# First GCN layer: bias from a table on VectorE, input split on GpSimd, transposes inside the first aggregation

## The chip, the cores and the metric

One core of a Trainium2 chip runs the whole program. The metric is device time in microseconds from launch to the last store. The profile is one execution of the program, recorded by the hardware. Engines are named as the profile names them: PE is TensorE, PEld its weight load, DVE is VectorE, ACT is ScalarE, POOL is GpSimd, SP issues DMAs.

## The reference, cut to what matters

The input is `x` of 32 graphs by 256 nodes by 128 features. A graph attention layer comes first, then a layer norm, two graph convolutions and four LSTMs over windows of 1 to 4 nodes, with a residual at each half.

```python
h = jnp.maximum(_layernorm(x, axis=-1), 0.0)
x = x + _L0_gnn_ref(h, adj, L0_gnn_W, L0_gnn_a)            # attention
h = jnp.maximum(_layernorm(x, axis=-1), 0.0)
# second half:
h = jax.nn.relu(jnp.einsum('ts,bsh->bth', adj, x @ Wg0 + bg0))
h = jax.nn.relu(jnp.einsum('ts,bsh->bth', adj, h @ Wg1 + bg1))
for p in range(1, 5):      # windows of p nodes: the last step's h replaces the window's last node
    last = _lstm_last(Wih[p - 1], Whh[p - 1], bih[p - 1], bhh[p - 1], wins)
    h = h.at[:, idx, :].set(last)
return x + h
```

In the first graph convolution the kernel aggregates before it multiplies: adj (v Wg0 + b0) is (adj v) Wg0 plus b0 times the row sums of adj. That last term, b0 by row sum, is the one the change handles in another way.

## The kernel before, in words

The 32 graphs go through in 16 pairs; one pair is 512 nodes, so most tiles are 128x512. Every engine has a hand-written program, run in order, and semaphores join them. The function `ticks` gives each engine a software pipeline: in tick t, stage s works on pair t - s. `live(s)` says whether that pair exists, and `after(...)` adds the wait for a buffer that is used again.

There are three parts. Part A (`phase_a`, to about 112 us of the profile) is attention. Part B (`phase_b`) holds the two graph convolutions and the LSTM with one step; its first four ticks run beside the end of part A, and ticks 4 to 21 alone (to about 230 us). Then the LSTMs with 2, 3 and 4 steps follow. fp32 products are made from a high and a low part of each operand (names ending in `_hi` and `_lo`), three products for one (`product`, L1005).

Part B by stages, for one pair:

- Stage 0: ACT normalises the pair into `v_norm` (`second_norm`, L545, four activations at L500). DVE makes its high part with a cast (L806) and its low part with a subtraction (L808).
- Stage 1, first aggregation: PE multiplies by the adjacency (twelve 256-column products). ACT copies the high part out of PSUM (`part_hi(1)`, L590), DVE subtracts for the low part (`part_lo(1)`, L792).
- Stage 2: PE multiplies by Wg0 and adds the bias by a fourth product, `b0_parts` by `rs_parts` (L1078). ACT applies relu for the high part, DVE makes the low part from PSUM (L794).
- Stage 3: PE multiplies by Wg1; ACT adds the second bias into `y1` (L597); PE transposes `y1` (`turned`, L1046 to L1055); high and low parts again.
- Stage 4, second aggregation, into `h_hi` (ACT, L590) and `h_lo` (DVE, L794).
- Stages 5 and 6: the one-step LSTM. PE computes three gates, ACT their activations (L573) and the tanh of the cell (L566). DVE computes the cell (L776), the output by three products of 168 or 176 columns (L768), its cast (L772) and its low part (L779).

The order within one tick of part B is this. PE: gates, stages 4, 3, 2, the transposes, stage 1. ACT: tanh, the gates I, G, O, high part 4, `y1`, high part 2, high part 3, normalisation, high part 1. DVE: L768, L772, L776, L779, low part 4, low part 2, low part 3, the input's cast and subtraction, low part 1.

GpSimd computes the norm's scale and shift for 16 tiles at a time (`norm_scale`), prepares the bias and row-sum operands, and splits the LSTM weights in 14 pieces of 256 columns (`split_weights`, L457). The last 12 pieces are paced by the LSTM's progress (L476).

```python
after(dve, b_mm[1], t, 0)
nc.vector.tensor_copy(s_hi[:, 0, :], v).then_inc(b_hi[0], 1)
dve.wait_ge(b_hi[0], t + 1)
nc.vector.tensor_tensor(s_lo[:, 0, :], v, s_hi[:, 0, :].bitcast(fp32),
                        ALU.subtract).then_inc(b_lo[0], 1)
```

Of the kernel before, what the change touches and what calls it, by code (L numbers as in the profile page):

```python
# [5 lines left out]
def preln_gat_gcn_lstm_kernel(  # L6
# [28 lines left out]
    P = 128  # L35
# [15 lines left out]
    GCN_LOADS = 8  # L51
# [7 lines left out]
    with ctx:  # L59
        def sb(name, shape, dt=fp32):  # L60
            return ctx.enter_context(nc.sbuf_tensor(name, shape, dt))
# [33 lines left out]
        b_raw = sb("b_raw", [P, D])  # L95
        b_full = sb("b_full", [P, D])
        b1_col = sb("b1_col", [P, 1])
        y1 = sb("y1", [P, 512])
        b0_parts = sb("b0_parts", [P, D], fp32r)
        rs_full = sb("rs_full", [P, N])  # L100
        rs_parts = sb("rs_parts", [P, 2, N], fp32r)
# [68 lines left out]
        b_zero = sem("b_zero")  # L170
# [3 lines left out]
        rs_ok = sem("rs_ok")  # L174
# [26 lines left out]
        b_y = sem("b_y")  # L201
        b_T = sem("b_T")
# [172 lines left out]
        def _(pool):  # L375
# [11 lines left out]
            done(nc.gpsimd.memset(b_raw[:, :], 0.0))  # L387
            nc.gpsimd.nop().then_inc(b_zero, 1)
# [39 lines left out]
            nc.gpsimd.nop().then_inc(rs_ok, 1)  # L428


            pool.wait_ge(gcn_w_in, GCN_LOADS * 16)
# [3 lines left out]
            nc.gpsimd.tensor_tensor(bl[:, :], bl_raw[:, 0], bl_raw[:, 1], ALU.add)  # L435
            done(nc.gpsimd.tensor_copy(b_full[:, :].bitcast(fp32r), b_raw[:, :]))
            done(nc.gpsimd.tensor_copy(b0_parts[0:32], b_full[0:32]))
            done(nc.gpsimd.tensor_tensor(b0_parts[32:64], b_raw[32:64], b_full[32:64], ALU.subtract))
            done(nc.gpsimd.tensor_copy(b0_parts[64:P], b_full[64:P]))
# [41 lines left out]
        def _(act):  # L481
# [80 lines left out]
            def phase_b(t, ph, live):  # L562
# [13 lines left out]
                def part_hi(s):  # L576
                    if not live(s):
                        return
                    if s == 4:
                        dst = h_hi[:, bass.ds((t - 4) * PN, PN)]  # L580
                    else:
                        dst = s_hi[:, s, :]
                    if s == 3:

                        act.wait_ge(b_T, t - 2)
                    else:
                        act.wait_ge(b_mm[s], t - s + 1)
                    if s < 4:
                        after(act, b_mm[s + 1], t - s, 0)
                    nc.scalar.activation(dst, ps[:, TURNED if s == 3 else s - 1, :],  # L590
                                         ACT.Copy if s in (1, 3) else ACT.Relu).then_inc(b_hi[s], 1)
# [67 lines left out]
        def _(dve):  # L659
# [97 lines left out]
            def phase_b(t, ph, live):  # L757
# [23 lines left out]
                def part_lo(s):  # L781
# [9 lines left out]
                    if s in (1, 3):  # L791
                        ins = nc.vector.tensor_tensor(dst, ps[:, TURNED if s == 3 else 0, :], hi.bitcast(fp32), ALU.subtract)  # L792
                    else:
                        ins = nc.vector.scalar_tensor_tensor(dst, ps[:, s - 1, :], 0.0, hi.bitcast(fp32), ALU.max,  # L794
                                                             ALU.subtract)
                    ins.then_inc(b_lo[s], 1)

                part_lo(4)
                part_lo(2)
                part_lo(3)  # L800
                if live(0):

                    v = v_norm[:, :, :].rearrange("p k f -> p (k f)")
                    dve.wait_ge(b_v, t + 1)
                    after(dve, b_mm[1], t, 0)
                    nc.vector.tensor_copy(s_hi[:, 0, :], v).then_inc(b_hi[0], 1)  # L806
                    dve.wait_ge(b_hi[0], t + 1)
                    nc.vector.tensor_tensor(s_lo[:, 0, :], v, s_hi[:, 0, :].bitcast(fp32),  # L808
                                            ALU.subtract).then_inc(b_lo[0], 1)
# [125 lines left out]
        def _(pe):  # L935
# [87 lines left out]
            def phase_b(t, ph, live):  # L1023
# [33 lines left out]
                for s in (4, 3, 2, 1):  # L1057
                    if s == 1:
                        turned()
                    if not live(s):  # L1060
                        continue
                    after(pe, b_y if s == 3 else b_lo[s], t - s, 0)
# [10 lines left out]
                    if s == 2:  # L1073

                        product(ps[:, s - 1, :], (wg_hi[:, 0, :], wg_lo[:, 0, :]), (hi, lo), True, False)
                        if isinstance(t, int) and t == 2:
                            pe.wait_ge(rs_ok, 1)
                        ins = nc.tensor.matmul(ps[:, s - 1, :], b0_parts[:, :], rs_parts[:, :, :].rearrange("p b n -> p (b n)"),  # L1078
                                               start=False, stop=True)
# [3 lines left out]
                    else:  # L1083

                        for b in range(2):
                            for u in range(2):
# [130 lines left out]
```

## Time and profile before

| | |
|---|---|
| median of 3 runs | 451.97 us (450.59 to 452.68) |
| the profiled execution, time | 452.38 us |
| its span | 450.5 us |
| mean granted TensorE clock | 0.992 |
| PE busy | 430.0 us (95%) |
| DVE busy | 374.5 us (83%) |
| ACT busy | 333.0 us (74%) |
| POOL busy | 71.5 us (16%) |

The span runs from the first to the last instruction; launch and end add 1.9 us to it. Busy shares are averages over three parts of the program. The matter of this case is a stretch of some 100 us in the middle, where all engines work in step on ticks.

### The profile page before, as it was taken

Reading aid. Unit: us, or ns where it says so; the run is one execution under the profiler, and the core shown is the slowest. Engines: PE = TensorE matmul, PEld = TensorE weight load, DVE = VectorE, ACT = ScalarE, POOL = GpSimd, SP = SyncE. Lnnn points to the kernel's source line nnn. Section 1 sums busy time; section 2 is a strip of 40 time slices with the busy share of each in tenths; the row PEclk is TensorE's granted clock in tenths of the full one; section 3 lists DMA queues with packets and bytes.
Section 4 is the critical chain, followed back from the end, with each engine's and each line's share of the span. In section 5 each row is a group of like instructions: output and inputs, shape, how many; then the busy total and the mean of one; then the engine's idle time right before and its main releaser. Section 6 shows DMA issues by size and latency. Waiting matters only on the chain.

```text
span 450.5 us, 7896 instructions
## 1 busy us (share of the span) xinstructions
PE 430.0 (95%) x2472; PEld 371.4 (82%) x2472; DVE 374.5 (83%) x973; ACT 333.0 (74%) x651; POOL 71.5 (16%) x169
## 2 busy tenths in 40 slices
PE   7689999979999999999999999999999999999995
PEld 6468888878888888888778888899999988887884
DVE  3898999997778877878778888878788789888995
ACT  2579999977899999997777768757767675574552
POOL 5848640422411213110000000000000000000000
PEclk9969999999999999999999999999999999999999
DMA  8910000000000000000000000000000000002116
GB/s 244 324 65 1 2 2 1 0 0 1 1 1 2 0 1 0 0 0 0 1 0 2 1 0 1 0 1 1 1 1 1 1 1 0 1 23 71 47 47 188
DMA packets 14213, 11.68 MB, mean 26 GB/s; under 512 B 1123, under 2 KB 12390, under 8 KB 13926
## 3 DMA queue, kind: packets, MB, share of 16 engines
q1 hardware_dynamic: 11542, 9.97, 7.3%
q10 hardware_dynamic: 2640, 1.33, 1.2%
q8 instruction: 16, 0.26, 0.2%
q14 instruction: 15, 0.12, 0.1%
HBM read 7.10 MB, written 4.19 MB: 25 GB/s over the span
## 4 chain that ended last, share of the span: by engine, by line
PE 70%; DVE 18%; ACT 5%; issue 3%; DMA 2%; DVEq 1%; SPq 0%; ACTq 0%
PE ps L1008 45%; PE ps L1152 12%; PE ps L1156 6%; DVE score L732 4%; DVE score L698 4%; DVE xs L746 2%; DMA xs<-in_x 2%; PE ps L1054 2%; DVE stats L688 2%; ACT v_norm L500 1%; DVE stats L665 1%; PE ps L988 1%; ACT work L625 1%; PE ps L1099 1%; PE ps L1078 1%
## 5 line engine op out<-in xcount | busy, mean ns | idle before, releaser
L625 ACT ACTIVATE work<-ps,bl 128x512 f32<-128x512 f32 (+2 forms) x204 | 111.0, 627 | 26.7 <-PE ps L1156 19.3
L1008 PE MATMUL ps<-h_hi,wl_hi 128*128 128x512 f32 (+3 forms) x252 | 93.5, 371 | 0.9 <-DVE xs L888 0.8
L1008 PE MATMUL ps<-h_hi,wl_lo 128*128 128x512 f32 (+3 forms) x252 | 92.8, 368 | 0.0
L1008 PE MATMUL ps<-h_lo,wl_hi 128*128 128x512 f32 (+3 forms) x252 | 92.7, 368 | 0.0
L615 ACT ACTIVATE work<-work 128x512 f32<-128x512 f32 (+2 forms) x56 | 31.5, 571 | 45.5 <-DVE work L883 34.6
L1008 PEld LDWEIGHTS ps<-h_hi,wl_hi 128*128 128x128 f32 x252 | 47.5, 188 | 8.3 <-issue 1.2
L500 ACT ACTIVATE v_norm<-xs,shift,scale 128x128 f32 (+1 forms) x128 | 53.3, 509 | 1.4 <-POOL shift L409 1.4
L1008 PEld LDWEIGHTS ps<-h_lo,wl_hi 128*128 128x128 f32 x252 | 47.4, 188 | 6.6
L1008 PEld LDWEIGHTS ps<-h_hi,wl_lo 128*128 128x128 f32 x252 | 47.5, 188 | 5.7
L1152 PE MATMUL ps<-s_hi,wl_hi 128*128 128x512 f32 (+2 forms) x144 | 51.7, 361 | 0.0
L1152 PE MATMUL ps<-s_hi,wl_lo 128*128 128x512 f32 (+2 forms) x144 | 51.2, 358 | 0.0
L573 ACT ACTIVATE work<-ps,bl 128x512 f32<-128x512 f32 x48 | 30.8, 683 | 6.5 <-DVE work L768 5.2
L988 PE MATMUL ps<-wh,pT 128*128 128x130 f32 x256 | 32.6, 280 | 2.8 <-DVE xs L746 2.1
L1156 PE MATMUL ps<-s_lo,wl_hi 128*128 128x512 f32 (+2 forms) x144 | 34.4, 358 | 0.3 <-DVE s_lo L845 0.3
L988 PEld LDWEIGHTS ps<-wh,pT 128*128 128x128 f32 x256 | 29.9, 190 | 5.6 <-ACT pT L542 3.6
L590 ACT ACTIVATE s_hi<-ps 128x512 fp32r<-128x512 f32 x48 | 28.1, 593 | 5.5 <-PE ps L1078 2.1
L834 DVE TENSOR_TENSOR s_hi<-work 128x512 fp32r<-128x512 f32 (+2 forms) x36 | 22.0, 611 | 12.0 <-ACT work L615 11.1
L533 ACT ACTIVATE prob<-score,ebias 128x256 f32<-128x256 f32 x64 | 28.0, 547 | 4.6 <-DVE ebias L710 4.6
L838 DVE TENSOR_TENSOR work<-work 128x512 f32<-128x512 f32 (+2 forms) x52 | 31.3, 602 | 0.0
L1152 PEld LDWEIGHTS ps<-s_hi,wl_hi 128*128 128x128 f32 x144 | 27.1, 188 | 3.0
L1152 PEld LDWEIGHTS ps<-s_hi,wl_lo 128*128 128x128 f32 x144 | 27.1, 188 | 2.9
L1156 PEld LDWEIGHTS ps<-s_lo,wl_hi 128*128 128x128 f32 x144 | 25.4, 188 | 3.7 <-DVE s_lo L845 0.6
(127 smaller groups left out, 924.5 us busy)
## 6 DMA issues: line engine op xcount, KB each, us to landing
result<-xs SPq DMA_DIRECT2D x12, 256.0 KB, 2.3
work<-in_w_ih_t SPq DMA_DIRECT2D x1, 1024.0 KB, 10.9
work<-in_w_hh_t SPq DMA_DIRECT2D x1, 1024.0 KB, 9.4
xs<-in_x SPq DMA_DIRECT2D x2, 256.0 KB, 3.6
xs<-in_x SPq DMA_DIRECT2D x1, 512.0 KB, 5.6
result<-xs SPq DMA_DIRECT2D x4, 128.0 KB, 2.4
result<-xs ACTq DMA_DIRECT2D x4, 128.0 KB, 2.8
adj_raw<-in_adj ACTq DMA_DIRECT2D x1, 256.0 KB, 6.8
```

The source lines that it names most:

```text
L500: ins = nc.scalar.activation(v_norm[:, k, :], xs[:, bass.ds(i, 1), :].rearrange("p o f -> p (o f)"), ACT.Relu, scale=scale[:, which, bass. ...
L533: ins = nc.scalar.activation(prob[:, m, k], score[:, m, k], ACT.Exp, scale=1.0 - SLOPE, bias=ebias[:, m, k:k + 1])
L573: nc.scalar.activation(one_row(g), ps[:, 4 + g, :], ACT.Tanh if g == G else ACT.Sigmoid, bias=bl[:, g:g + 1]).then_inc(one_act, 1)
L590: nc.scalar.activation(dst, ps[:, TURNED if s == 3 else s - 1, :], ACT.Copy if s in (1, 3) else ACT.Relu).then_inc(b_hi[s], 1)
L615: nc.scalar.activation(lw[:, par, R_TC, 0:cols], lw[:, par, R_C, 0:cols], ACT.Tanh).then_inc(c_act[par], 1)
L625: nc.scalar.activation(lw[:, par, g, 0:cols], ps[:, 4 * par + g, 0:cols], ACT.Tanh if g == G else ACT.Sigmoid, bias=bl[:, (p - 1) * GATES ...
L834: nc.vector.tensor_tensor(hi, shaped(lw[:, par, O, :]), shaped(lw[:, par, R_TC, :]), ALU.mult).then_inc(c_hi[par], 1)
L838: nc.vector.tensor_tensor(row(r, par, R_H), row(r, par, O), row(r, par, R_TC), ALU.mult).then_inc(c_h[par], 1)
L988: ins = nc.tensor.matmul(psA[:, b, ui * (D + 2):(ui + 1) * (D + 2)], pT[:, 2 * b + uj, ui * P:(ui + 1) * P], wh[:, (ph - 4) % 4, 2 * b + u ...
L1008: ins = nc.tensor.matmul(dst, a, b, start=start and n_ == 0, stop=stop and n_ == 2)
L1152: nc.tensor.matmul(ps[:, 4 * par + g, 0:cols], part, s_hi[:, par, 0:cols], start=False, stop=False)
L1156: nc.tensor.matmul(ps[:, 4 * par + g, 0:cols], weights(p, 1, g)[0], s_lo[:, par, 0:cols], start=False, stop=True).then_inc(c_gate[par], 1)
```

## The change

The bias of the first graph convolution leaves TensorE. GpSimd multiplies the row sums (already the same in every partition) by the bias, one value in each partition, to a table `b0_rs` of 128x256. In each tick DVE adds the table to the product in PSUM, in two halves of 256 columns, and writes `z0`, in SBUF. ACT's high part and DVE's low part of stage 2 now read `z0`. The split of `v_norm` moves from DVE to GpSimd, where it stands between the norm's scales and the pieces of the weights, whose pacing changes. The transposes of stage 3 move from before the first aggregation to its middle, after the first graph of the pair.

```diff
-            sp.wait_ge(b_zero, 1)
-            for r in (0, 32, 64):
-                sp.dma_start(b_raw[r:r + 1, :], b_gcn0.rearrange("(o f) -> o f", o=1)).then_inc(gcn_w_in, 16)
+            sp.dma_start(b0_col[:, :], b_gcn0.rearrange("(f o) -> f o", o=1)).then_inc(gcn_w_in, 16)
...
             pool.wait_ge(rs_read, 1)
-            done(nc.gpsimd.tensor_copy(rs_full[:, :].bitcast(fp32r), rs_raw[:, :]))
-            for b in range(2):
-                done(nc.gpsimd.tensor_copy(rs_parts[0:64, b], rs_full[0:64]))
-                done(nc.gpsimd.tensor_copy(rs_parts[96:P, b], rs_full[96:P]))
-                done(nc.gpsimd.tensor_tensor(rs_parts[64:96, b], rs_raw[64:96], rs_full[64:96], ALU.subtract))
...
+            nc.gpsimd.tensor_scalar(b0_rs[:, :], rs_raw[:, :], b0_col[:, 0:1], 0.0, ALU.mult, ALU.add).then_inc(b0_rs_ok, 1)
...
-            for c in range(4):
+            def second_scale(c):
                 pool.wait_ge(stats_ok, TILES + (c + 1) * QUARTER)
                 norm_scale(1, c * QUARTER, QUARTER)
-            for n_, (p, m, c) in enumerate((p, m, c) for p in range(2, SKIPS + 1) for m in range(2) for c in range(2)):
-                pool.wait_ge(one_lo, 1 + 3 * n_ // 4)
-                split_weights(p, m, c)
+            def input_parts(q):
+
+                v = v_norm[:, :, :].rearrange("p k f -> p (k f)")
+                pool.wait_ge(b_v, q + 1)
+                if q > 0:
+                    pool.wait_ge(b_mm[1], q)
+                done(nc.gpsimd.tensor_copy(s_hi[:, 0, :], v))
+                nc.gpsimd.tensor_tensor(s_lo[:, 0, :], v, s_hi[:, 0, :].bitcast(fp32), ALU.subtract).then_inc(b_lo[0], 1)
+
+            second_scale(0)
+            second_scale(1)
+
+            pieces = [(p, m, c) for p in range(2, SKIPS + 1) for m in range(2) for c in range(2)]
+            for q in range(PAIRS):
+                input_parts(q)
+                if q in (1, 5):
+                    second_scale(2 + q // 4)
+                for n_, piece in enumerate(pieces):
+                    if 7 + 3 * n_ // 4 == q:
+                        split_weights(*piece)
...
+                    elif s == 2:
+                        act.wait_ge(b_z, t - 1)
...
                 part_lo(4)
+                if live(2):
+
+                    dve.wait_ge(b_mm[2], t - 1)
+                    if isinstance(t, int) and t == 2:
+                        dve.wait_ge(b0_rs_ok, 1)
+                    after(dve, b_lo[2], t - 2, 0)
+                    for b in range(2):
+                        c = slice(b * N, (b + 1) * N)
+                        ins = nc.vector.tensor_tensor(z0[:, c], ps[:, 1, c], b0_rs[:, :], ALU.add)
+                    ins.then_inc(b_z, 1)
                 part_lo(2)
                 part_lo(3)
-                if live(0):
-
-                    v = v_norm[:, :, :].rearrange("p k f -> p (k f)")
-                    dve.wait_ge(b_v, t + 1)
-                    after(dve, b_mm[1], t, 0)
-                    nc.vector.tensor_copy(s_hi[:, 0, :], v).then_inc(b_hi[0], 1)
-                    dve.wait_ge(b_hi[0], t + 1)
-                    nc.vector.tensor_tensor(s_lo[:, 0, :], v, s_hi[:, 0, :].bitcast(fp32),
-                                            ALU.subtract).then_inc(b_lo[0], 1)
                 part_lo(1)
...
-                        product(ps[:, s - 1, :], (wg_hi[:, 0, :], wg_lo[:, 0, :]), (hi, lo), True, False)
-                        if isinstance(t, int) and t == 2:
-                            pe.wait_ge(rs_ok, 1)
-                        ins = nc.tensor.matmul(ps[:, s - 1, :], b0_parts[:, :], rs_parts[:, :, :].rearrange("p b n -> p (b n)"),
-                                               start=False, stop=True)
+                        ins = product(ps[:, s - 1, :], (wg_hi[:, 0, :], wg_lo[:, 0, :]), (hi, lo), True, True)
...
                         for b in range(2):
+                            if (s, b) == (1, 1):
+                                turned()
```

## Rows read from the trace of the kernel before

**Rows 1.** The page, part 4: the chain that ended last, by engine.

```profile
PE 70%; DVE 18%; ACT 5%; issue 3%; DMA 2%; DVEq 1%; SPq 0%; ACTq 0%
```

**Rows 2.** Busy us by engine (count), clock, DMA: eleven ticks of part B.

```profile
126.64:206.43 79.79, 79.42 (x485) 68.04 (x485) 65.72 (x133) 72.80 (x144) 13.64 (x24) 1.00 0.00 1
```

**Rows 3.** Timeline of PE in one tick of part B (start us, us).

```profile
162.90 0.66 PE L1054 MATMUL ps<-ident,y 128*128 128x128 f32 x4
...
169.50 0.39 PE L1008 MATMUL ps<-s_lo,wg_hi 128*128 128x512 f32 x1
169.73 0.40 PE L1078 MATMUL ps<-rs_parts,b_parts 128*128 128x512 f32 x1
170.15 0.66 PE L1054 MATMUL ps<-ident,y 128*128 128x128 f32 x4
```

**Rows 4.** Timeline of PEld, same tick; in brackets idle time and its releaser.

```profile
170.15 0.42 PEld L1054 LDWEIGHTS ps<-ident,y 128*128 128x128 f32 x4 [0.46 <-ACT y L597]
```

**Rows 5.** Timeline of ACT, same tick.

```profile
164.09 1.64 ACT L500 ACTIVATE v_norm<-xs,shift,scale 128x128 f32 x4
165.63 0.58 ACT L590 ACTIVATE s_hi<-ps 128x512 fp32r<-128x512 f32 x1
166.11 0.62 ACT L566 ACTIVATE work<-work 128x512 f32<-128x512 f32 x1
...
168.93 0.59 ACT L590 ACTIVATE h_hi<-ps 128x512 f32 x1
169.41 0.69 ACT L597 ACTIVATE y<-ps,b_col 128x512 f32<-128x512 f32 x1
```

**Rows 6.** Timeline of DVE, same tick.

```profile
165.76 0.43 DVE L806 CAST s_hi<-v_norm 128x512 fp32r<-128x512 f32 x1 [0.84 <-ACT v_norm L500]
166.22 0.69 DVE L808 TENSOR_TENSOR s_lo<-v_norm,s_hi 128x512 fp32r<-128x512 f32 x1
166.83 0.68 DVE L792 TENSOR_TENSOR s_lo<-ps,s_hi 128x512 fp32r<-128x512 f32 x1
167.43 0.82 DVE L768 TENSOR_TENSOR work<-work 128x176 f32<-128x176 f32 x3
168.40 0.43 DVE L772 CAST h_hi<-work 128x512 f32 x1
168.74 0.68 DVE L776 TENSOR_TENSOR work<-work 128x512 f32<-128x512 f32 x1
```

**Rows 7.** Line L732, 64 instructions: duration in ns, min/median/max.

```profile
L732 DVE SCALAR_TENSOR_TENSOR score<-ps,wh,score x64: 460/476/486, 17.5 to 97.6; 128x256 f32<-128x256 f32 x64
```

**Rows 8.** Timeline of POOL: a cast and a subtraction of 512 columns.

```profile
21.29 0.61 POOL L417 CAST adjT_hi<-adjT_raw 128x512 fp32r<-128x512 f32 x1
21.98 1.26 POOL L418 TENSOR_TENSOR adjT_lo<-adjT_raw,adjT_hi 128x512 fp32r<-128x512 f32 x1
```

**Rows 9.** Timeline of DVE at the same time.

```profile
22.18 1.08 DVE L706 SCALAR_TENSOR_TENSOR low<-m,wh 128x4 f32<-128x4 f32 x1
```

**Rows 10.** Line L706, 16 instructions: duration in ns, min/median/max.

```profile
L706 DVE SCALAR_TENSOR_TENSOR low<-m,wh x16: 151/166/1078, 22.2 to 100.5; 128x4 f32<-128x4 f32 x16
```

**Rows 11.** Groups by line of POOL: pieces of the LSTM weights (busy, mean ns).

```profile
L461 POOL TENSOR_TENSOR wl_lo<-work,wl_hi 128x256 fp32r<-128x256 f32 x14 | 10.3, 738 | 1.1
...
L460 POOL CAST wl_hi<-work 128x256 fp32r<-128x256 f32 x14 | 5.6, 397 | 54.6 <-DVE h_lo L779 54.2 <-POOL adjP_lo L452 0.2
```

**Rows 12.** Timeline of POOL: first and last of ten instructions of one `norm_scale`.

```profile
118.84 0.24 POOL L400 TENSOR_TENSOR ln_b<-stats 128x16 f32<-128x16 f32 x1 [14.17 <-DVE stats L688]
...
123.92 0.22 POOL L409 TENSOR_TENSOR shift<-ln_c,scale 128x16 f32<-128x16 f32 x1
```

**Rows 13.** Timeline of ACT: the normalisation of pair 1.

```profile
103.53 1.63 ACT L500 ACTIVATE v_norm<-xs,shift,scale 128x128 f32<-128x128 f32 x4
```

**Rows 14.** Timeline of PE in tick 3: transposes, then first aggregation.

```profile
113.32 0.60 PE L1054 MATMUL ps<-ident,y 128*128 128x128 f32 x4
113.67 0.36 PE L1008 MATMUL ps<-adjT_hi,s_hi 128*128 128x256 f32 x1
```

More of the change, by code:

```diff
@@ L50, in preln_gat_gcn_lstm_kernel @@
     SKIPS = 4
-    GCN_LOADS = 8
+    GCN_LOADS = 6
     GATES = 4
@@ L94, in preln_gat_gcn_lstm_kernel @@
         wg_lo = sb("wg_lo", [P, 2, D], fp32r)
-        b_raw = sb("b_raw", [P, D])
-        b_full = sb("b_full", [P, D])
+        b0_col = sb("b0_col", [P, 1])
         b1_col = sb("b1_col", [P, 1])
+        b0_rs = sb("b0_rs", [P, N])
+        z0 = sb("z0", [P, 512])
         y1 = sb("y1", [P, 512])
-        b0_parts = sb("b0_parts", [P, D], fp32r)
-        rs_full = sb("rs_full", [P, N])
-        rs_parts = sb("rs_parts", [P, 2, N], fp32r)
         ones = sb("ones", [P, P], fp32r)
@@ L169, in preln_gat_gcn_lstm_kernel @@
         pool_step = sem("pool_step")
-        b_zero = sem("b_zero")
         ones_ok = sem("ones_ok")
@@ L173, in preln_gat_gcn_lstm_kernel @@
         rs_read = sem("rs_read")
-        rs_ok = sem("rs_ok")
+        b0_rs_ok = sem("b0_rs_ok")
         adjT_ok = sem("adjT_ok")
@@ L201, in preln_gat_gcn_lstm_kernel @@
         b_y = sem("b_y")
+        b_z = sem("b_z")
         b_T = sem("b_T")
@@ L386, in _ @@
                                     pattern=[[-1, P]], channel_multiplier=1).then_inc(ident_ok, 1)
-            done(nc.gpsimd.memset(b_raw[:, :], 0.0))
-            nc.gpsimd.nop().then_inc(b_zero, 1)
             nc.gpsimd.memset(wh[:, :, :, D + 2:D + 3], 1.0)
@@ L422, in _ @@
             pool.wait_ge(rs_read, 1)
-            done(nc.gpsimd.tensor_copy(rs_full[:, :].bitcast(fp32r), rs_raw[:, :]))
-            for b in range(2):
-                done(nc.gpsimd.tensor_copy(rs_parts[0:64, b], rs_full[0:64]))
-                done(nc.gpsimd.tensor_copy(rs_parts[96:P, b], rs_full[96:P]))
-                done(nc.gpsimd.tensor_tensor(rs_parts[64:96, b], rs_raw[64:96], rs_full[64:96], ALU.subtract))
-            nc.gpsimd.nop().then_inc(rs_ok, 1)
             pool.wait_ge(gcn_w_in, GCN_LOADS * 16)
+            nc.gpsimd.tensor_scalar(b0_rs[:, :], rs_raw[:, :], b0_col[:, 0:1], 0.0, ALU.mult, ALU.add).then_inc(b0_rs_ok, 1)
             done(nc.gpsimd.tensor_copy(wg_hi[:, :, :], wg_raw[:, :, :]))
@@ L434, in _ @@
             nc.gpsimd.tensor_copy(ident_r[:, :], ident[:, :])
[L435 to L439, printed above, removed]
+            done(nc.gpsimd.tensor_tensor(bl[:, :], bl_raw[:, 0], bl_raw[:, 1], ALU.add))
             nc.gpsimd.nop().then_inc(b_ok, 1)
@@ L589, in part_hi @@
                         after(act, b_mm[s + 1], t - s, 0)
-                    nc.scalar.activation(dst, ps[:, TURNED if s == 3 else s - 1, :],
+                    nc.scalar.activation(dst, z0[:, :] if s == 2 else ps[:, TURNED if s == 3 else s - 1, :],
                                          ACT.Copy if s in (1, 3) else ACT.Relu).then_inc(b_hi[s], 1)
@@ L793, in part_lo @@
                     else:
-                        ins = nc.vector.scalar_tensor_tensor(dst, ps[:, s - 1, :], 0.0, hi.bitcast(fp32), ALU.max,
-                                                             ALU.subtract)
+                        ins = nc.vector.scalar_tensor_tensor(dst, z0[:, :] if s == 2 else ps[:, s - 1, :], 0.0,
+                                                             hi.bitcast(fp32), ALU.max, ALU.subtract)
                     ins.then_inc(b_lo[s], 1)
                 part_lo(4)
+                if live(2):
[7 more added lines that the diff above has]
+                    ins.then_inc(b_z, 1)
                 part_lo(2)
                 part_lo(3)
-                if live(0):
-                    v = v_norm[:, :, :].rearrange("p k f -> p (k f)")
-                    dve.wait_ge(b_v, t + 1)
-                    after(dve, b_mm[1], t, 0)
-                    nc.vector.tensor_copy(s_hi[:, 0, :], v).then_inc(b_hi[0], 1)
-                    dve.wait_ge(b_hi[0], t + 1)
-                    nc.vector.tensor_tensor(s_lo[:, 0, :], v, s_hi[:, 0, :].bitcast(fp32),
-                                            ALU.subtract).then_inc(b_lo[0], 1)
                 part_lo(1)
@@ L1057, in phase_b @@
                 for s in (4, 3, 2, 1):
-                    if s == 1:
-                        turned()
                     if not live(s):
+                        if s == 1:
+                            turned()
                         continue
-                    after(pe, b_y if s == 3 else b_lo[s], t - s, 0)
+                    after(pe, {2: b_z, 3: b_y}.get(s, b_lo[s]), t - s, 0)
                     if isinstance(t, int) and t == s:
@@ L1085, in phase_b @@
                         for b in range(2):
+                            if (s, b) == (1, 1):
+                                turned()
                             for u in range(2):
```

## The prediction

> **What bounds the kernel now.** I read the page's chain of waits first: PE holds 70% of it [rows 1]. The chain in order of time then shows a stretch from 126.64 to 206.43 us in which it never leaves PE but for one short wait a tick. That stretch is eleven ticks of part B, 79.79 us, so 7.25 a tick; PE is busy 79.42 of it, ACT 72.80, DVE 65.72, POOL 13.64, and the granted clock is full [rows 2]. PE is the bound, but ACT is only 0.6 us a tick behind it, so the order of the waits matters more than any busy share. Last I read one tick engine by engine.
>
> On PE the transposes start 7.25 us apart [rows 3]. Products of 512 columns start 0.23 apart, so after the bias product at 169.73 the transposes could start at 169.96; they start at 170.15, released by ACT's `y1` [rows 3, 4]. So the tick holds one bias product (0.23) and a wait of 0.19. ACT goes almost without a stop. DVE waits 0.84 for the normalisation before its cast, then casts and subtracts [rows 6].
>
> **The change part by part.**
>
> *Bias product removed, 16 times.* PE gives back 0.23 a tick. *Transposes moved behind half of the aggregation.* They get some 0.7 us more before PE needs `y1`, so the 0.19 goes as well. On PE alone the tick would be 7.25 - 0.23 - 0.19 = 6.83. That is the gain that is on offer.
>
> *Split leaves DVE.* The cast and the subtraction hold DVE from 165.76 to 166.83, 1.07 us a tick [rows 6], and the 0.84 us wait goes with them.
>
> *The sum z0 enters DVE.* Two instructions of 256 columns. Instructions of 512 columns start 0.61 apart (166.22 to 166.83) and three of 176 take 0.82, 0.27 each [rows 6]; by columns between them a 256 costs 0.35. Upper bound: L732 of that width lasts 0.476 with a tail of some 0.09, 0.39 [rows 7]; lower bound 0.27, the narrower one. I take 2 x 0.35 = 0.70, plus 0.09 for the last write and 0.07 to wake ACT: 0.86.
>
> *What z0 does to the order.* This is the step that decides. Before, ACT's high part 2 waited for PE only. Now it waits for DVE's z0, which stands in DVE's queue behind L768, L772, L776, L779 and low part 4. And behind the waiting instruction in ACT's queue stand high part 3, the normalisation, high part 1 and, in the next tick, the tanh, for which DVE's L768 waits. So a loop closes once a tick through ACT and DVE. I walk it, with 0 where ACT starts high part 2:
>
> - 0.97 normalisation starts (two high parts of 0.48, from 168.93 to 169.41 [rows 5]). It lasts 1.64, ends 2.61; high part 1 starts after 1.54, at 2.51 [rows 5].
> - 3.00 tanh starts (0.48 later [rows 5]), ends 3.62. High part 1 has ended at 3.09, so DVE's low part 1 runs from 3.13 to 3.74, and L768 could start then.
> - From L768 to L772 it takes 0.97, to L776 0.34 [rows 6]; then L776, L779 and low part 4 at 0.61 each, 1.83; then z0, 0.86: together 4.00.
> - The loop is 3.74 + 4.00 = 7.74, against the 7.25 of before: plus 0.49 a tick. PE's 6.83 isn't reached, it now waits 0.9 us a tick.
>
> So the removed product and wait are worth nothing here: their cover was PE as the bound, and it no longer is.
>
> *The split on GpSimd.* The trace has both instructions at that width: cast 0.61, subtraction 1.26, and 0.69 from start to start, so 1.95 together [rows 8]. It starts when the normalisation ends: 2.65 to 4.60 in the walk. PE needs the result for the aggregation at about 5; that alone would be hidden. But while GpSimd's subtraction ran from 21.98 to 23.24, a DVE instruction with 4 columns and two operands in SBUF took 1.08 us, to 23.26, where the median of its kind is 0.166 [rows 8 to 10]. It waited for the end of GpSimd's instruction. L768 has two SBUF operands too, and wants to start at 3.74, with GpSimd's subtraction under way until 4.60. So it comes 0.86 later, inside the loop: 8.60 a tick, plus 1.35. The bounds of this term are 0 (no collision) and the whole 1.26.
>
> The Trainium skill, "SBUF — State Buffer", section "Who interferes with whom", says that a VectorE instruction with two SBUF inputs contends with a GpSimd instruction that reads SBUF, and that whoever issues first blocks the other fully. By that rule the sum is the one just made; without it, the walk's 7.74. The trace agrees, in the one instance of [rows 9].
>
> *Eleven ticks.* 11 x 1.35 = 14.9 us.
>
> *Pieces of the weights.* Twelve pieces of 0.40 + 0.74 = 1.14 us [rows 11] stood where DVE read PSUM; now they stand right behind the split, while DVE runs L768, L772, L776 and L779, all SBUF work. If the two engines take turns, each piece delays DVE by its whole 1.14, 13.7 us in sum; if DVE, once on, keeps GpSimd out, by 0. I take half, 0.57 each: 6.8 us. No row shows who wins when both queue, so both ends stay in the range.
>
> *Scales moved behind the split of pairs 1 and 5.* One `norm_scale` takes 118.84 to 124.14, 5.3 us [rows 12]. Pair 1 is normalised at 105.16 [rows 13], its split ends at 107.2, the scale at 112.5, so pair 2's split at 114.5. Before, its aggregation started at 113.67 behind the transposes [rows 14]; now half of it has to come before the transposes, which move from 113.32 to 114.6 + 0.7 = 115.3. The chain through `y1`, high part 3 and the normalisation follows: plus 2.0 us, once (bounds 0, if the later ticks win it back, and 3). For pair 5 a tick is 8.6 us, and scale and split (7.3) fit in it: 0.
>
> *Preparation.* GpSimd's bias and row-sum copies, the memset and two of SP's DMAs go, and one multiplication comes. They lie before 50 us, where GpSimd then idles: 0. SP no longer waits for the memset, and nothing of weight stands behind that wait: 0. The last pieces end one tick later than before, with four ticks to spare: 0. Ticks 17 to 21 lose their normalisation and with it most of the loop: 0.
>
> **Sum.** 452.38 + 14.9 + 6.8 + 2.0 = 476.1 for the profiled execution, which lies 0.41 above the median of the runs: 475.7 us.
>
> **The rivals.**
>
> *A. No collision, only the longer loop.* GpSimd's split would slip by DVE, as GpSimd's instructions of 16 columns may. 11 x 0.49 = 5.4 and 2.0 at the start: 459.4. For it: only one row shows DVE held, and on a tiny instruction. Against it: that row's end agrees with GpSimd's end to 0.02 us.
>
> *B. PE stays the bound, and the kernel is faster.* By busy time it would be: DVE loses 1.07 and gains 0.70, ACT keeps its 6.6, PE needs 6.83. Eleven ticks of -0.42 are -4.6: 447.4. It decides if z0 starts before L779 has ended, or if the loop sums to less than 7.25, that is if my links are 0.49 too long. Against it: both queues run in order, and each link is a row.
>
> *C. Nothing moves.* Links shorter by 0.3 to 0.5 and the start won back: 452.
>
> *D. Turns taken at every boundary.* Each piece costs 1.14, and PE, idle a fifth of the time, perhaps loses clock: 483 and up. In the stretch shown the clock is full [rows 2], but there PE hardly idles.
>
> **How the numbers follow.** The forecast with its collision (466 to 482) 0.58; A 0.19; B 0.08; C 0.06; D 0.09. The range that holds 8 in 10 takes in A and leaves out B, C and half of D: 456 to 484. A change of under 0.5% (2.3 us) can't be told from none here. Faster 0.08, same 0.07, slower 0.85.
>
> **What the next profile would show.** Ticks (from transpose to transpose) of about 7.7 us if A, 8.6 before pair 7's tick and more with pieces if the forecast holds, 6.8 if B. ACT idle before high part 2 with DVE as releaser, about a microsecond, shows the loop. L768 far over 0.82 us for its three, with its end behind GpSimd's subtraction, shows the collision; L768 at 0.82 refutes it. GpSimd's cast and subtraction should stay near 0.61 and 1.26, if GpSimd is the one that comes first. PE should wait for `y1` and for stage 0's low part no longer than the loop makes it. I am wrong altogether if ACT's high part 2 starts as soon as PE is done.

## The result, and the profile after

Runs of both kernels alternated on one chip. The kernel after takes 480.49 us (median of 4 runs, 478.69 to 484.93), the kernel before 451.36 us (median of 4, 450.59 to 452.68). The ratio is 1.0627, 95% interval 1.0585 to 1.067: slower by 29 us. The forecast was 475.7 us, range 456 to 484, so it was 4.8 us too low and inside its range.

The profiled execution of after took 478.69 us, its span is 476.9 us and its mean granted clock 0.981. Against the profiled execution of before it is 26.3 us longer (26.4 in the span). It is the fastest of its four runs, so the steps below, which are taken from it, sum to somewhat less than the medians show.

From the page of after: the span, the engines' busy time (share, instructions), and the chain of waits by engine.

```profile
span 476.9 us, 7875 instructions
...
PE 430.3 (90%) x2456; PEld 369.8 (78%) x2456; DVE 386.5 (81%) x973; ACT 332.4 (70%) x651; POOL 98.4 (21%) x190
...
PE 46%; DVE 26%; issue 10%; ACT 10%; DMA 2%; POOL 2%; ACTq 1%; DVEq 1%; SPq 0%; POOLq 0%
```

PE is busy as long as before (430.0), but holds only 46% of the chain, where it held 70% [rows 1]. So what was added is waiting. The view of waits of after says where (engine and line that waited, for which; us in all, times, longest):

```profile
ACT s_hi L592 <- DVE z L809: 21.4, 16, 2.6
...
PE ps L1057 <- ACT y L599: 20.9, 13, 2.3
ACT work L573 <- DVE work L770: 15.1, 11, 1.5
```

This is the loop that the forecast walked: ACT's high part 2 waits for DVE's `z0`, an activation waits for DVE's three products, and PE waits for ACT's `y1`. (Lines after the change: L770 was L768, L774 L772, L778 L776, L781 L779, L796 and L794 are the low parts, L809 is `z0`, L592 the high parts, L599 `y1`, L1057 the transposes, L464 and L465 GpSimd's split, L444 and L445 the pieces.)

The same eleven ticks as in [rows 2], from the transposes of tick 5 to those of tick 16. The columns are as there (busy us of PE, PEld, DVE, ACT, POOL, then the clock):

```profile
128.76:230.57 101.81, 82.36 (x473) 70.42 (x474) 79.41 (x133) 72.10 (x143) 41.01 (x56) 0.95 0.00 0
```

They take 101.81 us instead of 79.79, so 22.0 of the 26.4 us are here, and PE is busy 82 of 102. Now one tick. The timeline of ACT in after:

```profile
174.92 0.63 ACT L592 ACTIVATE s_hi<-z 128x512 fp32r<-128x512 f32 x1 [1.23 <-DVE z L809]
175.46 0.58 ACT L592 ACTIVATE s_hi<-ps 128x512 fp32r<-128x512 f32 x1
175.93 1.64 ACT L500 ACTIVATE v_norm<-xs,shift,scale 128x128 f32 x4
177.47 0.58 ACT L592 ACTIVATE s_hi<-ps 128x512 fp32r<-128x512 f32 x1
177.95 0.63 ACT L566 ACTIVATE work<-work 128x512 f32<-128x512 f32 x1
...
184.74 0.63 ACT L592 ACTIVATE s_hi<-z 128x512 fp32r<-128x512 f32 x1 [1.76 <-DVE z L809]
```

The timeline of DVE in the same tick:

```profile
178.09 0.69 DVE L794 TENSOR_TENSOR s_lo<-ps,s_hi 128x512 fp32r<-128x512 f32 x1 [1.22 <-ACT s_hi L592]
178.70 2.44 DVE L770 TENSOR_TENSOR work<-work 128x176 f32<-128x176 f32 x3
181.29 0.43 DVE L774 CAST h_hi<-work 128x512 f32 x1
181.63 1.21 DVE L778 TENSOR_TENSOR work<-work 128x512 f32<-128x512 f32 x1
...
183.97 0.74 DVE L809 TENSOR_TENSOR z<-ps,b_rs 128x256 f32<-128x256 f32 x2
```

And that of GpSimd:

```profile
177.70 0.61 POOL L464 CAST s_hi<-v_norm 128x512 fp32r<-128x512 f32 x1 [6.05 <-ACT v_norm L500]
178.39 1.29 POOL L465 TENSOR_TENSOR s_lo<-v_norm,s_hi 128x512 fp32r<-128x512 f32 x1
179.63 0.51 POOL L444 CAST wl_hi<-work 128x256 fp32r<-128x256 f32 x1
180.22 0.73 POOL L445 TENSOR_TENSOR wl_lo<-work,wl_hi 128x256 fp32r<-128x256 f32 x1
181.01 0.40 POOL L444 CAST wl_hi<-work 128x256 fp32r<-128x256 f32 x1
181.49 0.81 POOL L445 TENSOR_TENSOR wl_lo<-work,wl_hi 128x256 fp32r<-128x256 f32 x1
```

Read the three side by side. From one high part 2 to the next is 9.82 us (174.92 to 184.74). ACT goes through its queue to the tanh at 177.95. DVE is free for L770 at 178.70, and its three products, 0.82 us before [rows 6], take 2.44. The first waits out GpSimd's subtraction (to 179.68). The other two come through one by one with GpSimd's next instructions: the group ends at 181.14, just after the first piece's subtraction at 180.95. L778 takes 1.21 instead of 0.68 beside the second piece. The engines take turns, an instruction of DVE between two of GpSimd.

PE's clock fell in some of these ticks, so it could be suspected too. Two ticks with one piece each, from one high part 2 to the next, settle it (columns as above):

```profile
165.61:174.92 9.31, 7.04 (x45) 5.99 (x44) 7.25 (x12) 6.56 (x14) 3.10 (x4) 1.00 0.00 1
213.16:222.45 9.29, 8.19 (x43) 6.99 (x42) 7.24 (x12) 6.55 (x13) 3.09 (x4) 0.83 0.00 0
```

At a granted clock of 1.00 and of 0.83 the tick is equally long. In all eleven ticks the way from high part 2 to DVE's first product is 3.77 to 3.78 us, and that from L781 to the next high part 2 is 1.97 to 1.98. Only the part between them, with L770 and L778, grows.

In a tick without a piece the two sides look like this (timeline of DVE, then of POOL, in after):

```profile
132.72 0.69 DVE L794 TENSOR_TENSOR s_lo<-ps,s_hi 128x512 fp32r<-128x512 f32 x1 [1.21 <-ACT s_hi L592]
133.33 1.72 DVE L770 TENSOR_TENSOR work<-work 128x176 f32<-128x176 f32 x3
```

```profile
132.96 1.30 POOL L465 TENSOR_TENSOR s_lo<-v_norm,s_hi 128x512 fp32r<-128x512 f32 x1
```

Here L770 takes 1.72, 0.90 more. From its start at 133.33 to the end of the subtraction at 134.26 it is 0.93.

### The profile page after: what moved, and what is told of

Same layout as the page of the kernel before. It is cut to its first block, busy times and chain, and to the rows that moved or that the text cites. A ratio compares the mean times of both kernels' runs of the same rounds, so it can differ in the third digit from the quotient of the medians.

```text
span 476.9 us, 7875 instructions
## 1 busy us (share of the span) xinstructions
PE 430.3 (90%) x2456; PEld 369.8 (78%) x2456; DVE 386.5 (81%) x973; ACT 332.4 (70%) x651; POOL 98.4 (21%) x190
## 4 chain that ended last, share of the span: by engine, by line
PE 46%; DVE 26%; issue 10%; ACT 10%; DMA 2%; POOL 2%; ACTq 1%; DVEq 1%; SPq 0%; POOLq 0%
PE ps L1011 26%; PE ps L1153 11%; PE ps L1157 5%; DVE score L734 4%; DVE work L770 4%; ACT v_norm L500 4%; DVE score L700 4%; DVE xs L748 2%; ACT s_hi L592 2%; DMA xs<-in_x 2%; DVE z L809 2%; DVE stats L690 2%; DVE stats L667 1%; ACT work L566 1%; ACT work L627 1%
## 5 line engine op out<-in xcount | busy, mean ns | idle before, releaser
L1011 PE MATMUL ps<-h_hi,wl_hi 128*128 128x512 f32 (+3 forms) x252 | 95.9, 380 | 0.9 <-DVE xs L891 0.8
L1011 PE MATMUL ps<-h_hi,wl_lo 128*128 128x512 f32 (+3 forms) x252 | 94.8, 376 | 0.0
L1011 PE MATMUL ps<-h_lo,wl_hi 128*128 128x512 f32 (+3 forms) x252 | 94.4, 375 | 0.0
L794 DVE TENSOR_TENSOR s_lo<-ps,s_hi 128x512 fp32r<-128x512 f32 x32 | 21.9, 688 | 22.3 <-ACT s_hi L592 22.3
L1057 PE MATMUL ps<-ident,y 128*128 128x128 f32 x64 | 11.5, 307 | 21.0 <-ACT y L599 20.9
```

The costliest lines, as they stand in the source:

```text
L1011: ins = nc.tensor.matmul(dst, a, b, start=start and n_ == 0, stop=stop and n_ == 2)
```

## The experiments

All ratios are to the kernel before on the same chip, with a 95% interval. "Tick" is the time from transpose to transpose. Where a run's eleven ticks are named, they are ticks 5 to 16, as above.

**Undo the split: DVE has it again, the pieces are paced as before (split_back).** The GpSimd function `input_parts` goes and DVE's block comes back:

```diff
-            for q in range(PAIRS):
-                input_parts(q)
...
+            for n_, (p, m, c) in enumerate((p, m, c) for p in range(2, SKIPS + 1) for m in range(2) for c in range(2)):
+                pool.wait_ge(one_lo, 1 + 3 * n_ // 4)
+                split_weights(p, m, c)
...
+                    nc.vector.tensor_copy(s_hi[:, 0, :], v).then_inc(b_hi[0], 1)
+                    dve.wait_ge(b_hi[0], t + 1)
+                    nc.vector.tensor_tensor(s_lo[:, 0, :], v, s_hi[:, 0, :].bitcast(fp32),
+                                            ALU.subtract).then_inc(b_lo[0], 1)
```

> The changed kernel with the split of the input back on VectorE and the pieces of the weights paced as before; the bias on VectorE and the transposes inside stay. Theory 1 (loop plus collision): L768's three products take 0.82 us again and the pieces cost nothing, but the loop through ScalarE and VectorE stays and now holds the cast and the subtraction too, between the end of the normalisation and low part 1. The walk gives 2.65 + 0.46 + 0.61 + 0.61 = 4.33 where L768 starts, and 4.00 on to the next turn: 8.3 us a tick, 11 x 1.08 = 12 and 1 to 3 at the start: 463 to 467 us. Rival (all of the loss is GpSimd's): 449 to 453 us, ticks of 7.25 or less.

Measured: 469.73 us (467.83 to 471.32), ratio 1.0378 [1.0339, 1.0417], ticks of 8.25 us. The timeline of DVE in split_back (its L754 is L768 of before):

```profile
165.20 0.43 DVE L802 CAST s_hi<-v_norm 128x512 fp32r<-128x512 f32 x1 [0.21 <-ACT v_norm L484]
...
166.87 0.82 DVE L754 TENSOR_TENSOR work<-work 128x176 f32<-128x176 f32 x3
```

The products are at 0.82 again, with no split and no piece of GpSimd beside them. Yet the tick is longer than before: `z0`, with DVE keeping the split, lengthens the loop by a microsecond, because all of it stands in one line. The ticks came out as expected; the time is 3 us over the range, and most of that is the end of the program, priced further down.

**The split alone, in the kernel before (split_alone).** GpSimd's new order is put into the kernel before, DVE's split goes, bias product and transposes stay.

> The kernel before with nothing changed but the split of the input and the order of the pieces, as in the changed kernel; the bias stays a product on TensorE. Theory 1: the collision works without z0 too, since GpSimd's split still follows the normalisation and L768 follows low part 1. Ticks about 8.0 us without a piece, 9 with one: 460 to 467 us. L768's three products take over 1.5 us. Rival (the split is free, z0's loop is the loss): VectorE has 1.07 us less a tick, TensorE stays the bound, 449 to 453 us.

Measured: 464.05 us (462.0 to 465.12), ratio 1.0238 [1.0191, 1.0286], ticks with pieces of 8.24 to 8.31. The timeline of POOL and DVE:

```profile
171.31 1.30 POOL L481 TENSOR_TENSOR s_lo<-v_norm,s_hi 128x512 fp32r<-128x512 f32 x1
171.62 2.44 DVE L784 TENSOR_TENSOR work<-work 128x176 f32<-128x176 f32 x3
172.54 0.51 POOL L460 CAST wl_hi<-work 128x256 fp32r<-128x256 f32 x1
173.14 0.74 POOL L461 TENSOR_TENSOR wl_lo<-work,wl_hi 128x256 fp32r<-128x256 f32 x1
```

The collision needs no `z0`. The split alone makes this kernel slower, and so do `z0` and the moved transposes without it (split_back).

**Half a subtraction (half_low).** If DVE waits for the end of GpSimd's subtraction, half the length must give back half of it. The low part of each pair's second graph is left out (it stays zero).

```diff
-                nc.gpsimd.tensor_tensor(s_lo[:, 0, :], v, s_hi[:, 0, :].bitcast(fp32), ALU.subtract).then_inc(b_lo[0], 1)
+                nc.gpsimd.tensor_tensor(s_lo[:, 0, 0:N], v[:, 0:N], s_hi[:, 0, 0:N].bitcast(fp32), ALU.subtract).then_inc(b_lo[0], 1)
```

> The changed kernel, but GpSimd's subtraction covers 256 of 512 columns (the low part of the second graph of each pair is left out as zero). Theory 1: that subtraction takes 0.73 instead of 1.29 us and ends 0.56 earlier, and L770's first product with it; every tick with a split and an L770 is 0.5 to 0.56 shorter: 12 x 0.55 = 6.6, so 473 to 475 us. Rival (VectorE and ScalarE's loop alone decides, the split lies beside it): 480 us, no change.

Measured: 471.96 us (471.11 to 473.08), ratio 1.0409 [1.037, 1.0449]. The subtraction takes 0.74 to 0.75, and the eleven ticks take 95.79 us, 6.0 less than in after, 0.55 a tick for an instruction 0.55 shorter. That is a microsecond better than I expected.

**Only writes (write_only).** The subtraction becomes a memset: GpSimd writes `s_lo` and reads nothing. The low part of the input is left out.

```diff
-                nc.gpsimd.tensor_tensor(s_lo[:, 0, :], v, s_hi[:, 0, :].bitcast(fp32), ALU.subtract).then_inc(b_lo[0], 1)
+                nc.gpsimd.memset(s_lo[:, 0, :].bitcast(fp32), 0.0).then_inc(b_lo[0], 1)
```

> The changed kernel, but GpSimd fills the input's low part with zeros and reads nothing (the low part of the input is left out). If GpSimd's reads are what VectorE's second operand waits for, L770's first product starts as soon as low part 1 is done, 0.9 us earlier, and only the piece's two instructions still hold it: 467 to 471 us, and in the ticks without pieces L770's three take 0.82. If writes collide just as well, the gain is only what the fill is shorter than the subtraction (1.29 us), and L770's first product still ends with GpSimd's fill.

Measured: 470.43 us (469.03 to 472.14), ratio 1.038 [1.0333, 1.0427]. The timeline of both engines in a tick without a piece:

```profile
141.93 0.53 POOL L465 MEMSET s_lo<- 128x512 f32 x1
142.27 0.83 DVE L770 TENSOR_TENSOR work<-work 128x176 f32<-128x176 f32 x3
```

DVE starts 0.19 us before the memset ends and takes its usual 0.83. The overlap is short here, but loop_only, below, has one tick in which the memset lies beside two of the three products, which start at 164.09:

```profile
164.06 0.53 POOL L465 MEMSET s_lo<- 128x512 f32 x1
```

They take 0.83 there too. In ticks with a piece DVE is still held. So it is GpSimd's reading of SBUF that holds DVE's instruction with two SBUF operands, and not its writing. The Trainium skill, "SBUF — State Buffer", section "Who interferes with whom", says that a VectorE instruction with two SBUF inputs contends with a GpSimd instruction that reads SBUF, and not with one that only writes it. The traces agree: held 0.90 us by an instruction that reads (the tick at 133.33 in after), not at all by one that only writes (loop_only at 164.09).

**Pieces moved out of the way (pieces_late).** Each tick's pieces wait until DVE has the LSTM's low part of that tick.

```diff
                     if 7 + 3 * n_ // 4 == q:
+                        pool.wait_ge(one_lo, q - 4)
                         split_weights(*piece)
```

> The changed kernel, but each piece of the weights also waits until VectorE has done L781 of the same tick, so that it runs beside instructions that read PSUM. Theory 1: the first two products of L770 are no longer held by pieces; ticks of 9.3 and 9.8 us fall to the 8.4 of ticks without one, 8.5 to 9 us in sum: 471 to 473 us. Rival (ticks grew for another reason, the loop's overhead): 480.

Measured: 472.24 us (470.11 to 474.05), ratio 1.0423 [1.0385, 1.0461]. Ticks with pieces take 8.53 us, but for one of 8.77, in which DVE's first product came just ahead of GpSimd's subtraction and the second was held.

**Only the loop (loop_only).** write_only and the wait of pieces_late together; the low part of the input is left out.

> The changed kernel with both collisions taken out: GpSimd fills the input's low part with zeros and reads nothing (the low part of the input is left out), and each piece of the weights waits for L781 of its tick. What is left is the loop through z0 alone, with L770's first product free of GpSimd. The walk of the prediction gave 7.74 us a tick; the two ticks without a piece in write_only were 7.4 and 7.6. So ticks of 7.4 to 7.7, 11 x 0.15 to 0.45 = 2 to 5 us, with 2 to 4 at the start and 2.3 after part B from the placement of h_hi: 459 to 463 us. If instead ticks stay over 8, the collisions aren't the rest of the loss; if they are 6.9, the loop is no bound.

Measured: 461.97 us (461.52 to 462.39), ratio 1.0203 [1.0161, 1.0246]. One tick on DVE, from L771 (after's L770) to the next low part 2:

```profile
164.09 0.83 DVE L771 TENSOR_TENSOR work<-work 128x176 f32<-128x176 f32 x3
...
166.61 0.68 DVE L797 SCALAR_TENSOR_TENSOR h_lo<-ps,h_hi 128x512 f32 x1
167.21 0.75 DVE L810 TENSOR_TENSOR z<-ps,b_rs 128x256 f32<-128x256 f32 x2
168.66 0.69 DVE L797 SCALAR_TENSOR_TENSOR s_lo<-z,s_hi 128x512 fp32r<-128x512 f32 x1 [0.70 <-ACT s_hi L593]
```

Here is the walk of the forecast without its collision: low part 2 comes at 160.97 in this tick and at 168.66 in the next, 7.69 apart, where the walk said 7.74.

The windows of the two kernels, each over its own same eleven ticks, loop_only first, then pieces_late:

```profile
128.78:212.92 84.14, 77.92 (x473) 66.64 (x474) 63.10 (x133) 71.12 (x143) 30.88 (x55) 1.00 0.00 0
```

```profile
128.06:221.59 93.53, 78.28 (x473) 66.37 (x473) 72.47 (x133) 72.12 (x143) 39.55 (x55) 1.00 0.00 0
```

They split the 22.0 us in three. From before (79.79) to loop_only (84.14): 4.4, the loop. From there to pieces_late (93.53): 9.4, the collision with the subtraction. From there to after (101.81): 8.3, where the pieces stand. The other way round it is nearly the same: the eleven ticks of write_only, with pieces and without the subtraction, take 92.72, so the pieces are 8.6 and the subtraction 9.1.

**The normalisation ahead of high part 2 (norm_first).** In ACT's queue the normalisation, for which GpSimd waits, goes ahead of the instruction that waits for `z0`.

```diff
-                part_hi(2)
-                part_hi(3)
                 if live(0) and not (isinstance(t, int) and t == 0):
...
                     second_norm(t)
+                part_hi(2)
+                part_hi(3)
                 part_hi(1)
```

> The changed kernel with the normalisation of the next pair ahead of high part 2 in ScalarE's queue, behind y1. Theory 1: the normalisation no longer waits for z0, it fills the microsecond or two in which ScalarE waited; GpSimd's split starts earlier and meets low part 4 and z0, which read PSUM. What is left of the loop is z0, two or three high parts, tanh, L770 and on: ticks fall by 1 to 1.5 us: 464 to 470 us. Rival (ScalarE's wait for z0 is slack): 480.

Measured: 460.48 us (458.6 to 462.38), ratio 1.0149 [1.0103, 1.0195], 20 us better than after and better than expected. The same two engines, in the order of their starts:

```profile
162.04 0.73 DVE L796 SCALAR_TENSOR_TENSOR s_lo<-z,s_hi 128x512 fp32r<-128x512 f32 x1 [0.89 <-ACT s_hi L592]
162.30 1.62 POOL L465 TENSOR_TENSOR s_lo<-v_norm,s_hi 128x512 fp32r<-128x512 f32 x1
162.69 1.28 DVE L794 TENSOR_TENSOR s_lo<-ps,s_hi 128x512 fp32r<-128x512 f32 x2
...
163.89 1.63 DVE L770 TENSOR_TENSOR work<-work 128x176 f32<-128x176 f32 x3
```

Here DVE came first, and GpSimd's subtraction takes 1.62 instead of 1.29: the hold works both ways. The rest of the subtraction lies beside DVE's two low parts from PSUM, which run at 0.6 each as always.

**The transposes alone (turn_alone).** In the kernel before, `turned()` moves between the two graphs of the first aggregation.

> The kernel before with the transposes inside the first aggregation, nothing else. By TensorE's own rows its wait of 0.19 us a tick for y1 goes: 11 x 0.19 = 2.1, so 449.5 where before is 451.5. By the walk the loop through VectorE is as long as the tick already (split and L768 to low part 4 behind the normalisation, and that behind high part 3, which the move delays by 0.5): no gain in the eleven ticks, and up to 1.4 lost in the first: 451 to 453. I expect the second.

Measured: 452.62 us (451.65 to 455.24, 10 runs), ratio 0.9998 [0.9972, 1.0025]. No change, and the tick stays 7.25 (135.00 to 142.25). PE gained nothing: `y1` comes later against PE's products too, and the transposes still wait for it. The timelines of PEld, ACT and DVE:

```profile
142.25 0.42 PEld L1054 LDWEIGHTS ps<-ident,y 128*128 128x128 f32 x4 [0.24 <-ACT y L597]
142.94 0.60 ACT L590 ACTIVATE s_hi<-ps 128x512 fp32r<-128x512 f32 x1 [0.26 <-PE ps L1054]
145.10 0.43 DVE L806 CAST s_hi<-v_norm 128x512 fp32r<-128x512 f32 x1 [0.84 <-ACT v_norm L500]
147.69 0.69 ACT L573 ACTIVATE work<-ps,bl 128x512 f32<-128x512 f32 x1 [0.46 <-DVE work L768]
```

They show a loop in which each link releases the next: the transposes (142.25), high part 3 of what they turned (142.94), the normalisation (143.44), DVE's split (145.10), low part 1 and L768 (146.78), the last gate (147.69), high part 4, `y1` (148.75) and the next transposes (149.50). That is 7.25 us, and of PE's products only the transposes are in it. The kernel before has the same links at the same distances: transposes 162.90, normalisation 164.09, cast 165.76, L768 167.43, `y1` 169.41, transposes 170.15 [rows 3, 5, 6]. So neither the 0.19 of [rows 4] nor the bias product, which isn't in the loop, was worth a shorter tick as long as this loop stood. The next tick of the kernel before (206.43 to 213.49), the first without a normalisation, takes 7.06, which is 7.25 less the wait of 0.19. This is read from the traces; no run shortens this loop alone.

**The end of the program, and where the buffers lie (pad, align64, before_off).** One difference was foreseen by nothing. From the transposes of tick 16 to the end of the span, before needs 244.07 us and after 246.33, though the code there is the same. The chains of before and of after show it in a group of 30 products, of which 20 read `h_hi` and 10 `h_lo` (start, us, line, count):

```profile
241.03 6.80 PE ps L1008 x30
```

```profile
265.38 7.00 PE ps L1011 x30
```

The products start 0.227 apart on average in one and 0.233 in the other. The change removes tensors ahead of `h_hi`, so that its address in SBUF moves from 162176 bytes, a multiple of 128, to 160672, which is 32 past one. Three kernels add a tensor of unused words ahead of `ones`, so that it and all behind it move: 383 words in after (meant to restore the old place, but the shift was 1504 bytes and the pad is 1532; `h_hi` came to 32 past a multiple again), 8 words in after (64 past), 8 words in before (32 past).

```diff
+        pad = sb("pad", [P, 8])
         ones = sb("ones", [P, P], fp32r)
```

> The changed kernel with an unused buffer of 383 words a partition ahead of `ones`, so that all buffers after it (h_hi, h_lo, ident and others) lie at the addresses of the kernel before; the change had shifted them by 1532 bytes. In the changed kernel's trace the LSTM rounds after part B are 2.3 us longer than before, with products of 512 columns that read h_hi starting 0.233 us apart where they were 0.227. Theory (addresses): they are back at 0.227, 2 to 3 us less: 477 to 479 us. Rival (clock, or state left by part B): 480 to 481, spacing 0.233.

> The changed kernel with an unused buffer of 8 words (32 bytes) a partition ahead of `ones`. The pad of 383 words had put h_hi 32 bytes past its old address: before it lay at a multiple of 64 bytes (162176), in the change (160672) and with that pad (162208) at an odd multiple of 32. Here it lies at 160704, a multiple of 64, elsewhere than before. Theory (alignment to 64 bytes): products of 512 columns that read h_hi in the two- and four-step rounds start 0.227 apart again, the stretch after part B is 2.3 us shorter: 477 to 479 us. Rival (only the old address would do, or something else in the change): 0.233, 480 to 481.

> The kernel before with the same 8 unused words, so that h_hi lies at 162208, an odd multiple of 32; nothing else differs. Theory (alignment): spacing 0.233 in the rounds after part B, 2 to 2.5 us more: 454.5 to 456 where before is 452 to 453.4. Rival: no difference.

Measured: pad 481.43 us (481.15 to 482.87), ratio 1.061 [1.0582, 1.0639]; align64 481.28 (478.51 to 482.72), 1.0611 [1.0567, 1.0656]; before_off 454.97 (452.91 to 457.42, 12 runs), 1.0053 [1.0028, 1.0078]. The same group in the chains of pad, align64 and before_off:

```profile
269.10 7.00 PE ps L1012 x30
```

```profile
268.81 6.88 PE ps L1012 x30
```

```profile
241.60 7.00 PE ps L1009 x30
```

The length follows the place: 6.80 at 0 past a multiple of 128, 6.88 at 64, 7.00 at 32, the last in either kernel. Eight unused words make the kernel before 2.5 us slower, which is the size of the difference at the end. The two pads in after missed what I expected of them, 477 to 479. The step to 64 didn't show in the time, whose runs spread over 4 us, but the traces have it: from the last transposes of part B to the end of the span it is 231.4 to 231.5 us in before, turn_alone and split_alone, whose buffers lie where before has them, 233.8 in after and in before_off, 234.2 in pad, and 232.7 in align64. So the place of the buffers makes the difference. Which buffer is open: `h_lo` moves by as much as `h_hi`, and products that read `s_hi`, which doesn't move, also go from 0.227 to 0.231 apart.

**A repair (repaired).** norm_first, the third quarter's scale one pair earlier, and 8 words.

> The changed kernel with three repairs together: the normalisation ahead of high part 2 (as in norm_first, 460.5 us), the scale of the third quarter behind pair 0's split instead of pair 1's, and the 8 unused words. The scale no longer stands ahead of pair 2's split: 2 to 3 us less at the start; alignment 2.3 less after part B: 455 to 457 us. It still can't beat the kernel before, since its ticks stay near 7.45 us.

Measured: 458.95 us (456.29 to 462.82), ratio 1.0143 [1.008, 1.0206]. The best form of the change, a little above what I expected, and still slower than before. Against norm_first its trace gains 2.0 us at the start and 1.0 at the end; the ticks, of 7.4 to 7.6, are the same.

## Why the prediction was right

The direction, the mechanism of the loss and its size were right; two terms were small, one was missing, and what the forecast said of the bound before was wrong. The terms of the sum in order, with what the profiles show:

| step | forecast, us | measured | from |
|---|---|---|---|
| the longer loop, 11 ticks | 5.4 | 4.4 | loop_only |
| subtraction holds L768, 11 ticks | 9.5 | 9.4 | pieces_late less loop_only |
| twelve pieces | 6.8 | 8.3 | after less pieces_late |
| start | 2.0 | 2.1 | tick at 128.76 against 126.64 |
| from tick 16 to the last low part of part B | 0 | -0.1 | 253.91 - 230.57 = 23.34 against 23.40 |
| the end of the program | 0 | 2.3 | from the last low part of part B: 222.99 against 220.67 |
| sum | 23.7 | 26.4 | spans |

*Bias product removed, transposes moved.* They gave nothing, as forecast, but not for the reason given. The forecast took PE for the bound, with 0.42 us a tick on offer. The tick of the kernel before was already set by a loop through PE's transposes, ACT and DVE (turn_alone), and neither part shortened it. PE's products filled the time to within 0.19 us, so that the busy share (95%) and the chain of waits (70%) named PE.

*The loop.* The walk gave 7.74 and loop_only shows 7.69. Its links hold: L771 starts 3.78 after high part 2 (walk 3.74), and from the start of `z0` to ACT it is 0.77 to 0.78, where I had 0.86. The two errors partly cancel. Rival A (459.4) would have been near without contention: loop_only measured 461.97, with over 2 us in it for the end of the program, which A hadn't counted.

*The split on GpSimd.* This was the step with the thinnest evidence, one instruction of 4 columns held for 1.08 us [rows 9]. Its size, 0.86 a tick, came out at 0.83 to 0.85. It rests on when DVE's product wants to start in relation to GpSimd's subtraction, which half_low and norm_first moved with the effect that this demands.

*Pieces.* I took 0.57 each, the middle between 0 and 1.14. It is 0.69 (8.3 / 12) to 0.72 (8.6 / 12): the engines take turns, so that most of a piece, but not all, lies in DVE's way. The middle was a guess, and that it came near was luck. The clock has no part in it: ticks with one piece are as long at 0.83 as at 1.00.

*Start.* That 2.1 agrees with 2.0 is luck. The attention of that execution ran ahead (a reciprocal in its DVE queue at 91.20, in before at 92.94, so 1.7 us early). From that reciprocal to the transposes of tick 5 it is 33.7 us in before, 37.6 in after, and 39.3 in pad and align64, which do the same work. So the change cost 3.9 to 5.6 there, and the term was too small. Of this 1.4 comes with the moved transposes alone (35.1 in turn_alone). Another part of the difference I had not seen: GpSimd's split also runs in the last ticks of part A and holds DVE there. The timeline of DVE and then of POOL in after:

```profile
93.15 0.94 DVE L712 SCALAR_TENSOR_TENSOR ebias<-m,low 128x4 f32<-128x4 f32 x1
```

```profile
92.80 1.27 POOL L465 TENSOR_TENSOR s_lo<-v_norm,s_hi 128x512 fp32r<-128x512 f32 x1
```

An instruction of 4 columns ends with GpSimd's, at 94.09 against 94.07, and ACT waited 0.75 us for it. In the profiled executions of the experiments with GpSimd's split the same tick began between 127.3 (split_alone) and 132.5 us (pad), so the start of a single profile can't be priced to a microsecond.

*The end of the program.* The forecast had nothing there. Code that the change doesn't touch got slower by 2.3 us; the same code lost 2.4 in before_off, by the place of the buffers alone.

*Rivals.* B fell with its condition, and with its premise that PE was the bound: `z0` starts behind L781 and low part 4 in every tick shown. C's shorter links were not found. D had the turns at every boundary right, but not the price of a piece, 1.14: it is 0.69 to 0.72. PE did lose clock, as D said, and it cost nothing in the ticks.

## What to carry to other kernels

A busy share of 95% doesn't make an engine the bound. Before work is moved between engines, walk one turn of the loop through the queues with starts and waits, before and after: here PE lost 0.23 us of work a tick that wasn't in the loop, and an added wait for the last of DVE's queue closed a longer one. Work for GpSimd that reads SBUF belongs beside DVE instructions with an operand in PSUM; beside DVE instructions with two operands in SBUF, whichever comes second waits out what is left of the first. When tensors are added or removed, compare a product far from the change in both traces: 32 bytes more ahead of the buffers cost this kernel 0.5%.

## What the runs showed of the hardware that was not expected

- When GpSimd and DVE both have instructions queued that want SBUF reads, they pass one by one: 3 products of 0.27 take 2.44 us beside a subtraction and a piece, 1.72 beside a subtraction alone.
- GpSimd's memset of 512 columns (0.53 us) doesn't hold DVE (0.83). Nor did every GpSimd instruction that reads SBUF: beside one of 16 columns that lasts 2.91 us (`scale<-ln_a,half`, at 137.24 in after), DVE's L796, with `z0` and `s_hi` in SBUF, started at 138.68 and took its usual 0.69.
- TensorE's products of 512 columns that read `h_hi` and `h_lo` start 0.227, 0.229 or 0.233 us apart on average when `h_hi` begins 0, 64 or 32 bytes past a multiple of 128. Other buffers move with it, and which one matters is open.
- With TensorE's granted clock at 0.83 a tick of 9.29 us was no longer than one of 9.31 at 1.00, since none of its products were in the loop.
